# Self-attention scores of a decoder block on both row halves of TensorE, with x loaded first

## What is computed

```python
x = _layernorm(x + _L0_attn_ref(x), axis=-1)
x = _layernorm(x + _L0_xattn_ref(x, ctx_4096, ctx_4096, Wq, Wk, Wv, Wo, bo, g), axis=-1)
x = _layernorm(x + _L0_ffn_ref(x, w_gate, w_up, w_down), axis=-1)
```

```python
q = jnp.transpose(x, (2, 0, 1))                              # l, n, c
scores = jnp.einsum('lnc,lmc->lnm', q, q) / 8.0
prob = jax.nn.softmax(scores, axis=-1)
msg = jnp.einsum('lnm,lmc->lnc', prob, q)
return x + jnp.transpose(msg, (1, 2, 0))
```

## Time and profile before

| | |
|---|---|
| median of 3 runs | 754.82 us (753.92 to 754.94) |
| the profiled execution | 753.69 us |
| its span in the trace | 751.9 us |
| PE busy | 692.3 us (92%) |
| DVE busy | 625.4 us (83%) |
| POOL busy | 527.0 us (70%) |
| ACT busy | 481.9 us (64%) |

### The profile page before, as it was taken

One profiled execution on the slowest core, in us unless ns is written; L12 is line 12 of the kernel. 1 busy time (PEld: TensorE's weight loads), 2 busy tenths in 40 slices (PEclk: granted clock), 3 DMA queues, 4 the chain that ended last, 5 costly groups with the idle time before them and its releaser, 6 DMA issues.

```text
span 751.9 us, 14539 instructions
## 1 busy us (share of the span) xinstructions
PE 692.3 (92%) x5520; PEld 392.5 (52%) x5520; DVE 625.4 (83%) x893; ACT 481.9 (64%) x869; POOL 527.0 (70%) x631
## 2 busy tenths in 40 slices
PE   0787799988999999999999999999999999999994
PEld 0787788834445445445445445445445454444552
DVE  1396996599888889899889889889888578999995
ACT  3139257477767767778778778777787644445544
POOL 3195474287868867888878878877777764747885
PEclk9999999999999999999999999999999999999999
DMA  9990012100000000001000000000000000001102
GB/s 310 162 226 2 2 30 71 30 15 0 2 29 2 28 2 30 28 1 31 28 2 30 25 5 29 2 29 25 25 2 1 1 1 1 15 29 43 43 15 85
DMA packets 21766, 26.95 MB, mean 36 GB/s; under 512 B 4033, under 2 KB 12225, under 8 KB 21697
## 3 DMA queue, kind: packets, MB, share of 16 engines
q1 hardware_dynamic: 21696, 26.02, 12.4%
HBM read 21.82 MB, written 4.19 MB: 35 GB/s over the span
## 4 chain that ended last, share of the span: by engine, by line
PE 64%; DVE 17%; POOL 6%; issue 5%; ACT 4%; DMA 2%; SPq 0%; POOLq 0%; DVEq 0%; ACTq 0%
PE banks L2518 8%; PE banks L2475 7%; PE banks L2555 7%; PE banks L2508 7%; PE banks L2532 7%; PE banks L2485 7%; PE banks L2460 5%; PE banks L2597 3%; PE banks L2443 3%; DVE big L876 2%; DMA big<-in_x_dram 2%; PE banks L2570 2%; DVE big L926 2%; ACT big L1703 2%; DVE big L881 2%
## 5 line engine op out<-in xcount | busy, mean ns | idle before, releaser
L1650 ACT ACTIVATE big<-banks 128x512 f32<-128x512 f32 (+3 forms) x352 | 199.5, 592 | 113.7 <-PE banks L2508 56.0
L527 POOL TENSOR_TENSOR big<-big 128x512 f32<-128x512 f32 x128 | 132.3, 1045 | 12.7 <-DVE big L976 12.7
L519 POOL TENSOR_TENSOR big<-big 128x512 f32<-128x512 f32 x64 | 87.2, 1368 | 20.1 <-ACT big L1720 19.9
L1715 ACT ACTIVATE big<-banks,big 128x512 f32<-128x512 f32 x128 | 87.3, 686 | 13.2 <-DVE big L956 11.4
L956 DVE TENSOR_REDUCE big<-banks 128x1 f32<-128x512 f32 x128 | 82.4, 676 | 14.5 <-PE banks L2475 14.1
L962 DVE TENSOR_REDUCE big<-banks 128x16 f32<-128x1024 f32 x64 | 77.3, 1208 | 17.2 <-PE banks L2485 16.8
L2518 PEld LDWEIGHTS banks<-ident,big 128*128 128x128 f32 x512 | 54.8, 141 | 69.2 <-ACT big L1650 41.4
L2508 PEld LDWEIGHTS banks<-ident,big 128*128 128x128 f32 x512 | 55.1, 141 | 64.4 <-issue 34.6
L2443 PE MATMUL banks<-big 64*32 64x32 f32 x1024 | 57.5, 441 | 28.2 <-ACT big L1650 20.8
L2508 PE MATMUL banks<-ident,big 128*128 128x128 f32 x512 | 81.2, 283 | 0.7 <-ACT big L1650 0.4
L967 DVE TENSOR_TENSOR big<-banks,big 128x1024 f32<-128x1024 f32 x64 | 77.9, 1217 | 2.5 <-PE banks L2518 1.1
(11 more groups left out here) (107 smaller groups left out, 1286.9 us busy)
## 6 DMA issues: line engine op xcount, KB each, us to landing
big<-in_x_dram SPq DMA_DIRECT2D x8, 1024.0 KB, 13.5
big<-in_ctx_dram SPq DMA_DIRECT2D x16, 256.0 KB, 2.9
out_dram<-big SPq DMA_DIRECT2D x16, 256.0 KB, 2.0
big<-in_L_ffn_w_down_dram SPq DMA_DIRECT2D x4, 688.0 KB, 10.6
big<-in_L_ffn_w_gate_dram SPq DMA_DIRECT2D x10, 256.0 KB, 2.6
big<-in_L_ffn_w_up_dram SPq DMA_DIRECT2D x10, 256.0 KB, 2.9
wg_area<-in_L_xattn_Wq_dram SPq DMA_DIRECT2D x2, 128.0 KB, 11.3
wg_area<-in_L_xattn_Wk_dram SPq DMA_DIRECT2D x2, 128.0 KB, 7.0
```

Source lines behind the costliest of these rows:

```text
L519: pool.tensor_tensor(qfold[:, i % 2], e[:, :, :, 0:DH // 2], e[:, :, :, DH // 2:DH], ALU.add).then_inc(s.q_folded, 1)
L527: pool.tensor_tensor(e, e, r, ALU.mult).then_inc(s.p_ready, 1)
L1650: return act.activation(dst, src, ACT.Copy)
L1715: act.activation(EK[:, f % 2, par, i], bank[par], ACT.Exp, bias=kneg[:, par, i:i + 1], accum_out=ksum[:, f % 2, par, i:i + 1]).then_inc(s. ...
```

## The change

Scores: of a column's four calls, j = 0 and 1 stay on partitions 0 to 63, and j = 2 and 3 read partitions 64 to 127. For that the upper half of xsw is filled too, with the even batches (swap_down, four VectorE copies of 64x2048, one per piece of x). In the upper partitions the order of the halves is reversed (odd batches first), so the moving operand reads them with a step of -1 and its columns come out in natural batch order either way; the output's rows for j = 2 and 3 come in the reversed order, and spread_probs reads them back with the halves exchanged. The bank stays the same one for all four calls. scores(0) also waits for swap_down. Loading: x is the first transfer; aw(0) follows it, and the first two items go behind aw(3). The written orders of all engines are new for the first two hundred calls or so, up to about the sixth pair; from there on they read as before.

```diff
-        x_even_odd = big[0:C, 0:2 * T * L].rearrange("p (n l) -> p n l", n=B)
-        x_by_batch = big[0:C, 0:2 * T * L].rearrange("p (s t l) -> p t s l", s=2, t=T)
+        both_x = big[:, 0:2 * T * L].rearrange("p (n l) -> p n l", n=B)
+        x_pairs = big[:, 0:2 * T * L].rearrange("p (s t l) -> p t s l", s=2, t=T)
+        x_by_batch = (x_pairs[0:C], x_pairs[C:P, :, ::-1])
...
-            load_aw(0)
-            for k in range(2):
-                load_item(k)
             for piece in range(4):
                 load_x(piece)
+            load_aw(0)
...
             for a in range(1, DN):
                 load_aw(a)
+            for k in range(2):
+                load_item(k)
             for t in range(2):
                 load_ctx(t)
...
+            def swap_down(piece):
+                dve.wait_ge(s.x_loaded[piece], 16)
+                dve.tensor_copy(xsw[C:P, 4 * piece:4 * piece + 4], xt[0:C, 4 * piece:4 * piece + 4]
+                                ).then_inc(s.swapped_down, 1)
...
+                p = pT[:, c % 3].rearrange("p l (s t) -> p l s t", s=2)
                 for j in range(4):
-                    last = act.activation(pd[:, c % 2, :, j], pT[:, c % 3], ACT.Identity, scale=quarter[:, j:j + 1], bias=zero[:])
+                    last = act.activation(pd[:, c % 2, :, j].rearrange("p l (s t) -> p l s t", s=2),
+                                          p if j < 2 else p[:, :, ::-1], ACT.Identity, scale=quarter[:, j:j + 1], bias=zero[:])
...
                 if c == 0:
                     pe.wait_ge(s.swapped_up, 4)
+                    pe.wait_ge(s.swapped_down, 4)
...
-                        last = pe.matmul(bank[c % 2][B * j:B * j + B, B * l:B * l + B], x_even_odd[:, :, at],
-                                         x_by_batch[:, :, :, at], start=True, stop=True)
+                        rows = slice(C * (j // 2), C * (j // 2) + C)
+                        last = pe.matmul(bank[c % 2][B * j:B * j + B, B * l:B * l + B], both_x[rows, :, at],
+                                         x_by_batch[j // 2][:, :, :, at], start=True, stop=True)
```

More of the change, by code:

```diff
@@ L1070, in out_stats @@
                 dve.bn_aggr(mv_o[:, u % 2], st_o[:, u % 2]).then_inc(s.ln_var, 1)
-            scale_item(0)
-            scale_item(1)
-            scale_aw(0)
-            shift_scores(0)
-            clip_aw(0)
[L1077 to L1082, removed]
+            swap_down(0)
+            swap_down(1)
+            swap_down(2)
+            swap_down(3)
+            shift_scores(0)
@@ L1128, in _ @@
+            k_max(0, 3, 1)
+            scale_aw(5)
+            clip_aw(3)
             add_msg(5, 1)
+            k_max(1, 0, 0)
+            k_max(1, 0, 1)
             add_msg(6, 0)
-            clip_aw(4)
-            k_max(1, 0, 0)
             add_msg(6, 1)
-            scale_aw(5)
             add_msg(7, 0)
@@ L1136, in _ @@
             x1_stats(0)
[L1137 to L1140, removed]
+            k_max(1, 1, 0)
+            k_max(1, 1, 1)
+            clip_aw(4)
+            dequant_item(0)
             q_max(0, 0)
             q_shift(0, 0)
-            k_max(1, 1, 0)
-            k_max(1, 1, 1)
+            scale_item(2)
             q_max(0, 1)
+            k_max(1, 2, 0)
             q_shift(0, 1)
@@ L1188, in _ @@
             k_max(2, 3, 0)
+            k_max(2, 3, 1)
+            clamp_ss(0)
+            dequant_item(1)
             scale_item(3)
@@ L1225, in _ @@
             norm_y(1)
+            dequant_item(2)
+            scale_g(2)
             scale_item(4)
-            scale_x(0)
-            scale_g(2)
             k_max(4, 0, 0)
             k_max(4, 0, 1)
-            x2_stats(1)
+            quantize_x(0)
             x1_stats(5)
@@ L1290, in _ @@
             x1_stats(7)
+            scale_x(2)
             q_max(6, 0)
@@ L1850, in _ @@
+            copy_down(1, 1)
             exp_k(1, 0, 0)
             exp_k(1, 0, 1)
+            copy_ctx(0)
+            copy_k(0, 0, 0)
+            norm_x1(0)
+            copy_k(0, 0, 1)
+            exp_k(1, 1, 0)
+            copy_down(2, 0)
+            exp_k(1, 1, 1)
+            copy_down(2, 1)
+            copy_k(0, 1, 0)
+            exp_q(0, 0)
             copy_k(0, 1, 1)
-            exp_q(0, 0)
             copy_k(0, 2, 0)
-            exp_k(1, 1, 0)
+            exp_k(1, 2, 0)
+            exp_q(0, 1)
@@ L2640, in _ @@
             messages(0, 1)
+            messages(1, 0)
+            messages(1, 1)
             transpose_down(0, 0)
             k_logits(0, 0)
-            messages(1, 0)
-            transpose_item(0)
-            transpose_down(0, 1)
-            messages(1, 1)
-            k_logits(0, 1)
-            transpose_down(1, 0)
             messages(2, 0)
             messages(2, 1)
-            transpose_down(1, 1)
+            k_logits(0, 1)
+            transpose_down(0, 1)
             messages(3, 0)
@@ L2661, in _ @@
             messages(6, 0)
-            transpose_down(2, 1)
-            k_logits(1, 0)
-            messages(6, 1)
-            messages(7, 0)
-            transpose_k(0, 0, 0)
-            messages(7, 1)
-            transpose_k(0, 0, 1)
-            transpose_ctx(0)
-            transpose_k(0, 1, 0)
-            transpose_down(3, 0)
-            transpose_k(0, 1, 1)
-            q_logits(0, 0)
-            transpose_k(0, 2, 0)
-            a_product(0, 0)
-            k_logits(1, 1)
+            transpose_down(1, 1)
@@ new lines, in _ @@
+            messages(6, 1)
+            k_logits(1, 0)
+            messages(7, 0)
+            messages(7, 1)
+            transpose_ctx(0)
+            k_logits(1, 1)
+            transpose_k(0, 0, 0)
+            transpose_k(0, 0, 1)
+            transpose_down(2, 0)
+            q_logits(0, 0)
+            transpose_down(2, 1)
+            a_product(0, 0)
+            transpose_k(0, 1, 0)
+            q_logits(0, 1)
+            k_logits(1, 2)
+            transpose_k(0, 1, 1)
+            transpose_k(0, 2, 0)
@@ L2677, in _ @@
+            a_product(0, 1)
+            transpose_down(3, 0)
+            transpose_item(0)
+            q_logits(0, 2)
             transpose_down(3, 1)
-            q_logits(0, 1)
-            a_product(0, 1)
             transpose_k(0, 2, 1)
+            k_logits(1, 3)
             transpose_k(0, 3, 0)
-            q_logits(0, 2)
-            k_logits(1, 2)
+            transpose_gu(0)
             transpose_k(0, 3, 1)
-            a_product(0, 2)
-            transpose_gu(0)
             q_logits(0, 3)
@@ L2701, in _ @@
-            q_logits(1, 2)
-            transpose_p(0, 1, 0)
+            q_logits(1, 1)
             a_product(1, 0)
             transpose_k(1, 2, 0)
+            transpose_p(0, 0, 0)
+            transpose_p(0, 1, 0)
+            transpose_p(0, 0, 1)
+            q_logits(1, 2)
+            y_product(0, 0)
+            k_logits(2, 1)
             a_product(1, 1)
-            transpose_p(0, 0, 1)
             transpose_p(0, 1, 1)
-            k_logits(2, 1)
+            transpose_p(0, 0, 2)
             q_logits(1, 3)
-            transpose_p(0, 0, 2)
@@ L2718, in _ @@
             transpose_p(0, 1, 3)
-            y_product(0, 2)
+            transpose_gu(2)
+            k_logits(2, 2)
+            y_product(0, 3)
             transpose_k(1, 3, 0)
-            transpose_gu(2)
-            y_product(0, 3)
+            q_logits(2, 1)
             transpose_k(1, 3, 1)
-            q_logits(2, 1)
+            a_product(1, 2)
             k_logits(2, 3)
             transpose_p(1, 0, 0)
+            sum_squares(0)
+            a_product(1, 3)
             transpose_p(1, 1, 0)
-            a_product(1, 2)
+            transpose_p(1, 0, 1)
@@ L2743, in _ @@
+            transpose_item(1)
+            k_logits(3, 0)
+            y_product(1, 0)
+            transpose_k(2, 0, 1)
+            q_logits(3, 0)
+            transpose_p(1, 0, 3)
             transpose_k(2, 1, 0)
-            q_logits(3, 0)
+            y_product(1, 1)
             a_product(2, 0)
-            transpose_p(1, 1, 2)
-            y_product(1, 0)
-            transpose_p(1, 0, 3)
             transpose_p(1, 1, 3)
+            y_product(1, 2)
             k_logits(3, 1)
             transpose_k(2, 1, 1)
-            y_product(1, 1)
+            q_logits(3, 1)
@@ L2776, in _ @@
             k_logits(4, 0)
+            g_product(2)
             transpose_p(2, 1, 2)
-            g_product(2)
             transpose_k(3, 0, 1)
```

437 lines of the change are left out of this document (193 added, 244 removed), and 21 rows, old and new, of the table first_groups.

## The result

The changed kernel takes 723.9 us (median of 4 runs, 723.3 to 725.1) against 754.4 of the kernel before in the same job: a ratio of 0.9604, 95% interval 0.9579 to 0.9629. The forecast was 726 in a range of 712 to 750. The profiled execution took 723.64 us with a span of 721.8, 30.1 us less than before.

What follows compares the result with a forecast made beforehand. PE was taken as the bound, with time saved before the messages start (96.60 us) saved at the end. Terms -3.2 - 31.2 + 5.8 + 1.0 = -27.6 took 753.7 to 726.1; forecast 726 us, range 712 to 750.

Steps and rivals of the forecast that it cites:

- What bounds it: Before the messages (96.60 us): time saved on PE there is saved at the end, if the following order keeps PE full.
- x first: Initial loads: three transfers move behind x, so PE starts at 17.6 instead of 20.8 us; -3.2, bounds 2.5 and 4.5.
- swap_down: VectorE's four copies beside ScalarE's during x's load: 1.25 to 2.35 us each, only the last can show; 0.1 taken.
- Scores: Eight score chunks ahead of the messages: two overlapping halves cut each from 7.2 to 3.3 us, ratio 0.46; -31.2.
- Gaps: PE's gaps between score chunks: late instruction blocks and waits put the messages at 68.0 instead of 62.2 us; +5.8.
- What is moved: VectorE and GpSimd work put behind the scores: +1.0, bounds 0 and 4; new order among tiles 0, bounds -2 and +6.
- B: Rival on the scores: no overlap because all four calls write one PSUM bank, chunks stay 7.2 us; 749.5 us, chance 0.14.
- C: Rival on the scores: each change of half on one bank drains the array, about 807 us; chance 0.07.
- D: Rival ahead of the messages: stalls vanish, instruction fetch keeps up, messages start at 48.9 us; about 707 us, chance 0.07.

Runs made afterwards that it cites:

- e1b: The changed kernel with all four score calls of a column back on partitions 0 to 63, run once more for its trace: 749.1 us.
- e2: The changed kernel with the loads in the old order (aw(0), first two items, then x): 732.3 us, ratio 0.9706 to the kernel before.
- e7: The changed kernel with shift_x(1) moved earlier on GpSimd and a column's four score calls in the order 0, 2, 1, 3: 717.3 us.
- e6: The changed kernel with scores reading neighbouring elements instead of operands with a 2 KB step (scores not those of the reference): 722.6 us in one run.
- e3: The changed kernel with shift_x(1) on GpSimd behind norm_p(4, 3, 1) instead of norm_p(5, 1, 1): 717.3 us, ratio 0.9515 to the kernel before.
- e1: The changed kernel with all four score calls of a column back on partitions 0 to 63: 748.3 us, ratio 0.9930 to the kernel before.
- e5: The changed kernel with the four xq transfers issued only after scores(7), a diagnosis: 746.4 us in a single run.

## Why the prediction was right, point by point

- *What bounds it.* Right. The messages start 31.95 us earlier and the span is 30.1 us shorter; e1b shows the same from the other side, 24.9 us at the messages and 25.5 in the span.
- *x first, -3.2.* PE's start moved by 4.3 us, inside the bounds; e2 shows that the term is 7 us in this kernel, since the late start also costs a late block of instructions. That part stood in the sum under the gaps.
- *swap_down.* 1.22 us each, just under the lower bound of 1.25, all hidden: the last ends at 15.74 us, ScalarE's last at 16.43.
- *Scores, 8 x (7.2 - 3.3) = -31.2.* Mis-sized: a chunk takes 3.85 us, a ratio of 0.53 where 0.46 was taken, so the term is -26.8. The pairs taken for the ratio did not bear it. g_product's 22 ns and project_b's 50 ns differ not only by alternation: project_b takes 1.62 us at 59.22 in the changed kernel, where the granted clock is half, and 0.98 us in e7 where it is full (next section). At equal clock the ratio is 0.70. Nor do their operands step 2 KB, which e6 shows to set the pace of the scores. The prediction had said beside it that two halves can give at most 0.5 where each is limited by itself, and then took 0.46, beyond that. Half the time, 3.6 us, holds within 0.25 us, and in e7 the order of calls changes nothing.
- *Gaps, +5.8.* Mis-sized the other way. Gaps add up to 17.4 us (64.65 - 16.48 - 8 x 3.85), not 24.0: -0.8. The mechanism was right: PE resumes after pairs 352, 480 and 608 at 30.1, 40.4 and 47.5 us, forecast 33, 41.5 and 50. Missed was that the next block (pair 736) still came by this road, at 53.7, and that blocks come 6 to 7 us apart once the wide rows follow xq. What the prediction calls gaps, 18.2 us before, includes 4.5 us of project, project_wo and project_b; the 17.4 include 3.4.
- *What is moved, +1.0, with bounds of -2 and +6 among the tiles.* The sum was near, 1.9 us lost between the messages and the end, but as a difference of two things. By the start of the sixth pair's queries the changed kernel is 36.7 us ahead (268.43 against 231.72), 4.8 more than at the messages; then 6.6 are lost at one place, shift_x(1). I had only a bound for such a thing and named the wrong stretch (up to the third pair); the written order of GpSimd beside VectorE's showed it, had I followed quantize_x(1) to its source. e3 prices it at 6.6 us.
- *The rivals.* B's time, 749.5, is near what e1 gives (748.3), without its cause: one PSUM bank does not keep the halves apart. C did not happen. D did not happen either: the stalls stay, and the messages start at 64.65, not 48.9. Even e6, without the stalls and with chunks of 1.93 us, starts them at 62.31, for want of instructions. The Trainium skill, page "TensorEngine Tiling (Array Packing)", section "Gotcha 1: PSUM Pressure", says that different row tiles cannot access the same PSUM bank simultaneously. Taken as a rule on time, this case does not show it: here the halves write the same bank in different partitions, and a chunk takes 3.85 us instead of 7.3. Halves that write the same partitions of one bank were not tried.
- The errors: +4.4 (scores), -6.6 (gaps), -1.1 (load), +0.9 (moved) make -2.4, and 726.1 - 2.4 is 723.7. That 726 came so near is luck: its two largest errors cancel. What bounds the kernel, and that the halves overlap on one bank, was right by its reasons.

## What to carry over

Where a small matmul reads one row half only, put half of the calls on the other half, even on the same PSUM bank if the partitions differ; it halved the time of the scores here, and the order of the calls did not matter. Then look at what feeds PE: here a stream of small DMA packets (180 GB/s) delayed PE's own instructions, and moving wide rows ahead of it was worth some 5 us more. When an order is rewritten by hand or by a planner, follow each moved call to the in-order engine that waits for it: one late call cost 6.6 us of the 36.7 gained.

## What the runs showed of the hardware

In the changed kernel the granted clock falls to half at 28.4 us, when PE has stood still since 27.8 for want of instructions, and stays there until about 66 us; the scores did not notice. An issue gap is not needed for it: in e5, which has none of a microsecond, the clock falls at 31.6 us, with PE busy but for 0.28 us at 29.0. Windows of the changed kernel, then of e7 (the last three numbers are clock, DMA share, GB/s):

```profile
25.00:27.80 2.80, 2.80 (x87) 2.64 (x87) 2.73 (x4) 1.58 (x1) 0.50 (x1) 1.00 1.20 180
30.10:34.00 3.90, 3.86 (x128) 3.72 (x128) 2.35 (x3) 0.00 (x0) 3.90 (x2) 0.50 1.18 180
```

```profile
61.00:64.70 3.70, 3.70 (x128) 3.68 (x128) 3.63 (x4) 3.69 (x2) 3.70 (x2) 1.00 0.02 4
...
59.96 0.98 PE L2374 MATMUL banks<-wg_area 64*64 64x64 f32 x32
```

A chunk takes 3.86 us at 1.2 GHz and 3.93 (from 60.87 us in e7) at 2.4. At 1.2 GHz the chunk of e6, with neighbouring elements, takes 1.93 (from 47.71 us, clock 0.50). So the reads set the pace of the scores, not the clock. project_b does notice: 1.62 us at 1.2 GHz, 0.98 at 2.4. It takes 1.61 us in the kernel before, where the profile shows a clock of 1.00 though no change of the clock is recorded ahead of 101 us; I take it that PE ran at 1.2 GHz there too, from its duration alone; no record shows it.

Bursts of scores, whose operands are read with wide steps, hold up ops of ScalarE, VectorE and GpSimd: 7.49 us for a ScalarE op of 0.63; in the changed kernel 3.09 for VectorE's subtraction of 0.69, and 3.97 for GpSimd's product L498 (at 47.39 us) of 1.05. Not every op is held, nor always to the end of the burst. The reduction L933, which reads PSUM and writes 16 columns, takes 0.69 us at 20.48, in the middle of the first burst. In e5 a reduction in SBUF (L940) ends at 31.27, beside a burst that lasts until 33.22. With neighbouring elements (e6) none of the ops looked at is held up. The Trainium skill, page "SBUF — State Buffer", section "SBUF: two separate sides", says that PE, ScalarE and VectorE's own pair never wait on anyone; ScalarE's 7.49 us against 0.63 do not agree, and e6 shows that the wide steps are the condition.
